# Reordering the attention rounds of a fused attention and expert layer on one core: norm rows before masking and low parts, row transposes before the sums' transpose, gate before the second keys, x before the mix

## What is computed

```python
# attention, 16 heads of 8, 32 random features per head
q, k, v = split(x @ w_qkv)
q_proj = elu1(q @ proj); k_proj = elu1(k @ proj)      # elu1(a) = a + 1 if a > 0 else exp(a)
kv = k_proj^T v ; z = 1 / (q_proj . k_proj.sum(tokens) + 1e-8)
x = layernorm(x + (q_proj kv * z) @ w_out + b_out)
# experts
gate = l2norm(x @ Wp^T) @ l2norm(sim)^T / temperature  # top 2 of 8, softmax over the two
x = layernorm(x + sum over the two: p * (gelu(x @ W1[e] + b1[e]) @ W2[e] + b2[e]))
```

## Time and profile before

| | us |
|---|---|
| median of three runs | 314.13 |
| the three runs | 314.13, 310.71, 314.23 |
| the profiled execution | 313.02 |
| its span, first to last instruction | 311.1 |
| TensorE busy in the span | 276.0 (89%) |
| VectorE busy | 212.4 (68%) |
| ScalarE busy | 190.9 (61%) |
| GpSimd busy | 176.1 (57%) |
| mean granted TensorE clock | 0.963 |

### The profile page before, as it was taken

How to read it: one execution, slowest core, us unless ns; L and a number is a source line. 1 busy time by engine, 2 the same in 40 slices (tenths; PEclk the granted TensorE clock), 3 DMA queues, 4 the chain that set the end, 5 groups by cost and what they waited for, 6 DMA issues and landing times.

```text
span 311.1 us, 8852 instructions
## 1 busy us (share of the span) xinstructions
PE 276.0 (89%) x2540; PEld 249.0 (80%) x2540; DVE 212.4 (68%) x837; ACT 190.9 (61%) x511; POOL 176.1 (57%) x207
## 2 busy tenths in 40 slices
PE   7699999999999999988999999999999999999600
PEld 6578787777768687766998899999999999999500
DVE  2466769697896999777575765445444588888761
ACT  5565758566666758555556555555555565888742
POOL 1500214666667666466526777777777547777730
PEclk9989999999999999999799999999999999999955
DMA  5990101101121002332101133333321644553140
GB/s 150 347 289 4 37 3 51 37 27 63 35 71 36 27 30 65 78 88 72 35 20 37 46 103 94 94 101 109 103 73 54 214 135 140 171 178 122 47 169 35
DMA packets 23556, 27.91 MB, mean 90 GB/s; under 512 B 4250, under 2 KB 16584, under 8 KB 23510
## 3 DMA queue, kind: packets, MB, share of 16 engines
q1 hardware_dynamic: 19190, 18.82, 21.0%
q0 software_dynamic: 4320, 8.53, 7.7%
HBM read 16.17 MB, written 11.62 MB: 89 GB/s over the span
## 4 chain that ended last, share of the span: by engine, by line
PE 27%; DVE 12%; issue 7%; DVEq 4%; POOL 4%; POOLq 0%; ACT 0%; ACTq 0%
PE pair L658 12%; PE bank L678 6%; PE pair L678 6%; DVEq L1122 3%; DVE w_t L1128 2%; DVE z L1299 2%; DVE z L1293 2%; PE pair L647 1%; DVE st L1305 1%; POOL routed_rows L389 1%; PE bank L580 1%; DVE y_sb L1282 1%; POOL rs L378 1%; DVE xtT L1116 1%; POOL expert_rows L412 1%
## 5 line engine op out<-in xcount | busy, mean ns | idle before, releaser
L906 ACT ACTIVATE h<-pair,w_t 128x128 f32<-128x128 f32 x284 | 81.2, 369 | 52.5 <-PE pair L658 51.7
L389 POOL DMA_INDIRECT routed_rows<-x,slot_of x64 | 67.1, 1049 | 44.6 <-issue 38.1
L412 POOL DMA_INDIRECT expert_rows<-y_sb,xt x71 | 71.9, 1013 | 30.9 <-issue 16.0
L658 PE MATMUL pair<-xtT,w_t 128*128 128x128 f32 x568 | 76.7, 278 | 1.2 <-DVE w_t L1128 1.2
L658 PEld LDWEIGHTS pair<-xtT,w_t 128*128 128x128 f32 x568 | 69.8, 194 | 2.6 <-DVE w_t L1128 2.5
L1128 DVE COPY w_t<-w_sb 128x516 f32 x71 | 31.0, 439 | 24.8 <-issue 24.4
L820 ACT ACTIVATE expo<-pair 128x1024 f32<-128x1024 f32 x32 | 32.8, 1026 | 20.4 <-PE pair L515 19.8
L678 PE MATMUL pair<-w_sb,h 128*128 x288 | 38.8, 278 | 0.4 <-ACT h L906 0.4
L678 PE MATMUL bank<-w_sb,h 128*128 x280 | 37.2, 276 | 0.0
L678 PEld LDWEIGHTS pair<-w_sb,h 128*128 128x128 f32 x288 | 35.5, 194 | 0.6 <-issue 0.6
L678 PEld LDWEIGHTS bank<-w_sb,h 128*128 128x128 f32 x280 | 34.4, 193 | 0.0
(11 more groups left out here) (202 smaller groups left out, 458.5 us busy)
## 6 DMA issues: line engine op xcount, KB each, us to landing
xt<-routed_rows SPq DMA_DIRECT2D x71, 66.0 KB, 2.0
yb<-expert_rows SPq DMA_DIRECT2D x7, 512.0 KB, 3.7
x_tok<-in_L_attn_x_dram SPq DMA_DIRECT2D x8, 256.0 KB, 2.9
w_sb<-in_L_ffn_W_dram SPq DMA_DIRECT2D x1, 2048.0 KB, 9.1
out_dram<-z SPq DMA_DIRECT2D x7, 256.0 KB, 2.0
expert_rows<-y_sb,xt POOLq DMA_INDIRECT x71, 2.3
routed_rows<-x,slot_of POOLq DMA_INDIRECT x64
routed_rows<-pad_rows SPq DMA_DIRECT2D x8, 66.0 KB
```

Of the source, the lines that this page charges most:

```text
L389: pool.indirect_dma_start(out=xs_dram, out_offset=bass.IndirectOffsetOnAxis(ap=slot_of[:, s, t, k:k + 1], axis=0), in_=x2[:, s * T + t, :] ...
L412: pool.indirect_dma_start(out=y_dram, out_offset=bass.IndirectOffsetOnAxis(ap=xt_u[:, i % XR, D:D + 1], axis=0), in_=y_sb[:, i % YR, :], i ...
L658: mm = nc.tensor.matmul(B[i % 2][:, cols(c)], w1_t[:, i % WR, cols(c)], xtT[:, i % 2, :], start=True, stop=True)
L906: ins = nc.scalar.activation(h[:, i % 2, cols(c)], B[i % 2][:, cols(c)], ACT.Gelu, bias=w1_t[:, i % WR, F + c:F + c + 1])
```

## The change

Five moves, no instruction added or removed:

1. VectorE, each round: `norm_rows(r)` comes first behind `features(s, 2)`, then `mask_key_values(s)`, then `x_low(s + 1)`. In the last round `take_tile(0)` stays ahead of all of them.
2. TensorE, each round: `transpose_x2(r)` stands right behind `values(s + 1)`, ahead of `transpose_sums(s)` and `keys(s + 1, 0, 0)`.
3. TensorE: `gate(q, *)` stands ahead of `keys(s, 0, 1)`.
4. TensorE: `transpose_x(s + 1)` stands ahead of `mix_heads(r)`.
5. ScalarE: `take_x2` stands ahead of `take_sums`, in the rounds and once behind them.

```diff
@@ TensorE
-                pe.wait_ge(s_kv_bd, s)
-                keys(s, 0, 1)
                 if q >= 0:
                     if s == 2:
                         pe.wait_ge(s_gw, 2)
                     gate(q, 0)
                     gate(q, 1)
-                else:
+
+                pe.wait_ge(s_kv_bd, s)
+                keys(s, 0, 1)
+                if q < 0:
                     fold_gate()
...
                 transpose_attn(r)
-                mix_heads(r)
                 if s + 1 < SEQS:
                     transpose_x(s + 1)
+                mix_heads(r)
                 queries(s, 1, 0)
...
                 if s + 1 < SEQS:
                     values(s + 1)
+                transpose_x2(r)
                 transpose_sums(s)
                 if s + 1 < SEQS:
                     keys(s + 1, 0, 0)
-                transpose_x2(r)
@@ ScalarE
                 r, q = s - 1, s - 2
-                take_sums(r)
                 if q >= 0:
                     take_x2(q)
+                take_sums(r)
...
+            take_x2(SEQS - 2)
             take_sums(SEQS - 1)
-            take_x2(SEQS - 2)
@@ VectorE
                 features(s, 2)
+                if s == SEQS - 1:
+                    take_tile(0)
+                norm_rows(r)
+                mask_key_values(s)
                 if s + 1 < SEQS:
                     x_low(s + 1)
-                if s == SEQS - 1:
-                    take_tile(0)
-                mask_key_values(s)
-                norm_rows(r)
                 if s == SEQS - 1:
                     take_tile(1)
                 features(s, 3)
```

## The result

The changed kernel takes 321.89 us (median of 4 runs, 319.6 to 323.01), the kernel before 313.66 (median of 4, 310.71 to 314.23): ratio 1.0273, 95% interval 1.0185 to 1.036. It is slower, by about 8 us. The profiled execution after is the fastest of its four, 319.6 us, with a span of 317.9 us, so the two spans differ by 6.8 us.

| stretch | before | after | e3_filled |
|---|---|---|---|
| start to first transposes | 31.36 | 31.42 | 31.95 |
| round 1 | 17.27 | 18.05 | 18.04 |
| round 2 | 17.51 | 18.21 | 18.20 |
| round 3 | 17.44 | 19.71 | 18.14 |
| round 4 | 17.44 | 19.76 | 18.14 |

A forecast was written before the change was run, and what follows sets the result against it. TensorE was taken to pace the round (busy 16.18 of 17.44 us). Five rounds at 0.8 us, +0.3 for the sixth and +0.1 for the last gave +4.4 on 313.6: 318.0 us, range 313.5 to 323.0.

The forecast's parts named there:

- the first rival: TensorE's clock falls in the new 2.2 us pause: two falls give 320.8 us, one in each of six 326; chance 0.20.
- The root stays where it is: GpSimd's root, seemingly held by the features, still ends at 72.93, so the norm rows start no earlier.
- The pause and the 0.8 us a round: TensorE idles 2.2 us ahead of the row transposes; numerators start 0.83 us later, taken as 0.8 a round, bounds 0.65 to 1.0.
- The wait of 0.1 us of keys (0,0) for `xT_lo`: On TensorE behind the sums' transpose: keys (0,0), ready at 74.83, wait for the low part until 74.93.
- x ahead of the mix is worth nothing: On TensorE, queries, sums and values come 0.35 us earlier, but the row transposes next in line wait anyway.
- The sixth round: Round near 130 us with a late scatter landing: slack takes up later numerators; +0.3 us, bounds -0.2 and +0.8.
- The last round, and the second part that shifts as a whole: ScalarE's sums' copies delay the table load under the numerators: 0.1 us, bounds 0 and 0.5; second part keeps its length.
- The case: The forecast itself, +4.4 us to 318.0 us, its own range 316.6 to 319.9; chance 0.55.
- The price of 1.4 us a fall: Loss on TensorE from a 3.5 us stretch at half the clock: at most 1.75 us, taken as 1.4.
- GpSimd did not become late: Rival: later features (s,3) delay iota and scatters, holding the root of the norms in five rounds; 322.7 us, chance 0.07.
- The loop over the scatters: Rival: the closed cycle over GpSimd sets the round, so the change costs 0 from five such rounds on; chance 0.10.
- The root freed by moving `x_low`: Rival: GpSimd's root ends 0.3 us earlier, at 72.6; a round costs 0.5, total 316.5 us; chance 0.08.

The follow-up runs named there:

- e3_filled: The changed kernel with eight unused matmuls of ident by ident ahead of the row transposes in rounds 1 to 6: 315.85 us, ratio 1.0063.
- e7_features_late: The kernel before with VectorE's features (s,2) moved behind the norm rows in the rounds: 311.81 us, ratio 0.9946.
- e5_gate_only: The kernel before with only the gate moved ahead of keys (0,1): 315.07 us, ratio 1.0076.
- e6_rows_only: The kernel before with only TensorE's row transposes moved right behind the values: 315.59 us, ratio 1.0079.
- e4_x_only: The kernel before with only the transposes of x moved ahead of the mix: 313.18 us, ratio 0.9985.
- e9_after_x_back: The changed kernel with one move undone, x transposed behind the mix again: 315.74 us, ratio 1.0072.
- e8_combined: The kernel before with features (s,2) behind the norm rows, x ahead of the mix and both GpSimd roots earlier in the queue: 319.32 us, ratio 1.0185.
- e2_dve_back: The changed kernel with VectorE's order as before, TensorE's and ScalarE's moves kept: 322.91 us, ratio 1.0281.
- e1_dve_only: The kernel before with only VectorE's order changed (norm rows, masking, low part): 327.81 us, ratio 1.0418.

## Why the prediction was right, and where it was wrong

The forecast was 318.0 us. The measured 321.89 lies inside the stated range of 313.5 to 323.0, but not by the case that the forecast describes: the hole came as forecast, but where the clock holds the whole change adds 2.1 us of span (e3_filled) and not 4.4, and falls of the clock, the first rival, add 4.7 more. That the time lies in the range is owed to that rival as much as to the forecast, and in part to luck: the sum was too high, and the falls, which it left out, brought it back and beyond.

*The root stays where it is.* Right. The norm rows start 2.25 us behind `ve` before and after, and e7_features_late shows why: without the features beside it the root takes 1.07 us. The argument that moving norm rows ahead of the masking can't bring them forward held to the hundredth. (The six waits of rows 2 are not quite of one length, as I wrote: the first is 0.22 us, and the first pause after is 1.94.)

*The pause and the 0.8 us a round.* Right in place and nearly in size: forecast a pause of 2.2, measured 2.10; forecast +0.83, taken as 0.8, measured 0.70 to 0.78 in the three rounds without a fall and 0.69 to 0.77 in e3_filled's first five, 3.6 us together against the 4.0 of the sum. From the row transposes to the numerators it forecast 77.52 - 74.31 = 3.21 us; the trace has 3.08. e5_gate_only and e6_rows_only confirm both halves of the chain. The wait of 0.1 us of keys (0,0) for `xT_lo`, named as a sign, didn't show.

*x ahead of the mix is worth nothing.* Right for time spent (e4_x_only), wrong for what follows. I priced the 0.35 us at zero because what came next waited anyway. It did wait; but it made that wait longer, and the length of the wait was not free.

*The sixth round.* Forecast +0.3. Without a fall it lasts 18.14 (e3_filled) against 18.47 before, so -0.33. The scatter's landing, for which the iota waited 2.68 us before, took its usual 1.44 in the trace after. In e5_gate_only it was late again (2.36) and the round lasted 18.14 all the same, so a late landing has slack in the longer round. Why it is late at times isn't shown.

*The last round, and the second part that shifts as a whole.* This term, 0.1 us, was mis-sized: from the last transposes to the end it gave back 1.30 us after and 1.73 in e3_filled. Most of it lies in the last round (s = 7): 18.59 us before, 17.07 in both of these. Before, the clock fell once behind the run of numerators (PEclk 0.72 between 150 and 156 us); after, it stayed 1.00 there. e9_after_x_back fell there too and has 18.72; e6_rows_only, with no fall, has 17.51. I saw no reason to count that fall as part of the time before, and it is. It isn't in every trace of the old order: e4_x_only's came 11 us earlier, from 140.2, and its last round took 17.09.

*The case.* The forecast was +4.4, for a clock that holds. The sum of e3_filled, where it holds, is 2.1 us of span: 3.2 in rounds 1 to 6, less 1.7 behind them, plus 0.6 in the opening. The changed kernel has three falls of 1.56 us in its profile, 4.7 us on top; its six rounds together add 8.04, and its span 6.8. That was the first rival, given 0.20, and it is the case that came, with three falls rather than two. The step that failed is the weight against it: "here transposes, keys and the gate follow it closely, and the round before kept 1.00 throughout". Closely following work didn't save the clock in three rounds of six, and a round with a 0.4 us pause says nothing of one with 2.1. The row that spoke for it, the 2.29 us pause in the opening, was the nearer in length and deserved the greater chance. The price of 1.4 us a fall was close. The range was drawn loosely: it was said to leave out three falls and more, but three falls at 1.4 us are 322.2, which lies inside it. A time above 320.4, as it came, had been given 0.21. The other three runs of the changed kernel are 2 to 3.4 us above the profiled one and had mean clocks of 0.943 to 0.948 against its 0.953; more falls would explain that (a fall of 3.4 us at half the clock lowers the mean over 318 us by 0.005), but they have no profile, so it isn't shown.

*The other rivals.* GpSimd did not become late: the iota waited 1.64 us in the round shown, and `scores` followed the key features without a wait. The loop over the scatters did not set the rounds. The root freed by moving `x_low` did not happen: after, the low part stands 2.7 us behind the root's start and the root takes 1.42 us all the same. But my reading of the rule was too weak. The Trainium skill (SBUF — State Buffer, "Who interferes with whom") says of a VectorE instruction with two SBUF inputs that it contends with a GpSimd instruction that reads SBUF. I took the last round as a sign that the low part doesn't hold the root. e8_combined shows that it does, when the root arrives while it runs (0.91 us from the low part's end to the root's), which agrees with the rule. Before, the root arrives during the features, and the low part that follows at once adds nothing: the root ends 0.90 us behind the features and 0.30 behind the low part.

## What to carry to other kernels

Before moving a step forward, find what releases it: if that is another engine's result, the move can't bring it forward and only pushes back whatever stood in its wait. Work standing in a wait is paid for already, and an order that puts two waits of one chain back to back on the bounding engine turns cover into a hole. On TensorE the length of a hole is a second price: taking 0.44 us of work away ahead of it made this kernel 6 us slower, and meaningless matmuls inside it made it 6 us faster, so a "free" saving ahead of a wait must be checked against the clock.

## What the runs showed of the hardware

Pauses of 1.50 to 1.68 us in this place left the granted clock at 1.00 in all twelve rounds of e6_rows_only and e9_after_x_back; pauses of 1.92 to 2.11 us lost it in three of six rounds of the changed kernel and four of six of e2_dve_back, each time for about 3.4 us at 1.2 GHz, which made the round 1.3 to 1.6 us longer. Which rounds lose it differs between kernels with the same pauses. The length of one pause doesn't decide alone: in e1_dve_only pauses of 1.68 to 1.71 us, each with one of 0.27 us soon behind it, lost it in four of six rounds, and single falls came behind no pause above 0.57 us in the kernel before (from 151.4 us), 0.67 us in e4_x_only and 0.49 us in e7_features_late. What else decides, no run here isolates. A GpSimd root asked for during a VectorE instruction with two SBUF inputs ends 0.90 to 0.92 us behind that instruction (features and low part alike; without one it takes about 1.05 us), and an indirect scatter issued during the features mostly 0.84 to 0.92 us behind them. In e8_combined two features in a row held a scatter through both; features with the low part right behind them held the root only through the features. Why the two differ isn't shown.
